# Two layer-norm and routing stages: half the normalization on ScalarE, a reordered addition, weight halves kept in DRAM, fewer filler products

## The reference, cut to what matters

```python
x = x + 0.5 * ffn(layernorm(x))          # "f1"
x = x + attention(layernorm(x))          # 16 heads of 8, relative positions
x = x + 0.5 * ffn(layernorm(x))          # "f2"

def ffn(x):
    normed = layernorm(x) * gamma + beta
    probs = softmax(normed @ router_w.T)             # 8 experts
    top_v, top_i = top_k(probs, 2); gates = softmax(top_v)
    out = sum over the 2 chosen experts of gate * (silu(g) * u) @ down_w[e].T   # 384 wide
    return out + shared_expert(normed)               # the same with 128, for every row
```

## Time and profile before

| | |
|---|---|
| median of 3 runs | 2171.59 us (2169.85 to 2174.17) |
| the profiled execution | 2175.47 us, of which the span 2173.70 us |
| TensorE busy | 2020.4 us (93%) |
| VectorE busy | 1906.4 us (88%) |
| ScalarE busy | 1292.8 us (59%) |
| GpSimd busy | 1257.7 us (58%) |
| mean granted clock of TensorE | 0.97 |

### The profile page before, as it was taken

How to read it: one execution, slowest core, us unless ns; L and a number is a source line. 1 busy time by engine, 2 the same in 40 slices (tenths; PEclk the granted TensorE clock), 3 DMA queues, 4 the chain that set the end, 5 groups by cost and what they waited for, 6 DMA issues and landing times. The chain is left out here.

```text
span 2173.7 us, 64335 instructions
## 1 busy us (share of the span) xinstructions
PE 2020.4 (93%) x22950; PEld 1228.5 (57%) x22951; DVE 1906.4 (88%) x4137; ACT 1292.8 (59%) x3126; POOL 1257.7 (58%) x1841
## 2 busy tenths in 40 slices
PE   7899999778999999999999999999999887999990
PEld 4589999533444444444444444444444465999990
DVE  7987666586999999999999999999999789877666
ACT  4455555376666666666666666666666354555550
POOL 3777775334555555556555555555565367777550
PEclk8999999899999999999999999999999899999995
DMA  5353222385021011202211210121000134322218
GB/s 165 91 134 88 86 83 64 105 258 143 2 41 41 7 36 41 39 4 41 41 29 14 41 41 7 36 60 41 2 7 7 56 106 130 105 88 85 72 50 234
DMA packets 163708, 147.86 MB, mean 68 GB/s; under 512 B 51858, under 2 KB 138002, under 8 KB 162898
## 3 DMA queue, kind: packets, MB, share of 16 engines
q1 hardware_dynamic: 144288, 108.31, 20.2%
q0 software_dynamic: 17280, 35.56, 4.8%
q10 hardware_dynamic: 1874, 0.51, 0.1%
HBM read 87.81 MB, written 60.45 MB: 68 GB/s over the span
## 5 line engine op out<-in xcount | busy, mean ns | idle before, releaser
L1330 PE MATMUL ps_scores<-c_relw,stat_rel 64*64 64x512 f32 x4096 | 937.4, 596 | 0.0
L1397 ACT ACTIVATE probs<-ps_scores,neg_max 128x512 f32<-128x512 f32 x1024 | 695.7, 684 | 396.1 <-DVE neg_max L1372 394.9
L1372 DVE TENSOR_REDUCE neg_max<-ps_scores 128x1 f32<-128x512 f32 x1024 | 645.4, 664 | 8.9 <-PE ps_scores L1330 7.9
L1365 DVE STREAM_TRANSPOSE probs_T<-probs 128x1024 f32<-128x1024 f32 x512 | 627.1, 1225 | 0.1
L1318 PE MATMUL ps_scores<-keys,stat_keys 64*64 64x512 f32 x2560 | 588.2, 595 | 0.5 <-ACT probs L1397 0.5
L1330 PEld LDWEIGHTS ps_scores<-c_relw,stat_rel 64*64 64x64 f32 x4096 | 278.5, 132 | 277.9 <-issue 209.3
L1318 PE MATMUL ps_scores<-c_batch,stat_keys 64*64 64x512 f32 x1536 | 352.6, 595 | 5.0 <-POOL stat_rel L1265 3.0
L1263 POOL TENSOR_TENSOR stat_keys<-queries_by_head,c_mask 128x128 f32<-128x128 f32 x320 | 152.5, 477 | 312.1 <-PE ps_scores L1330 312.1
L1290 PEld LDWEIGHTS ps_values<-probs_T,values_diag 128*32 128x32 f32 x8192 | 208.2, 109 | 205.3 <-issue 204.0
L1290 PE MATMUL ps_values<-probs_T,values_diag 128*32 128x128 f32 x8192 | 276.1, 276 | 1.1 <-DVE probs_T L1365 1.1
L1318 PEld LDWEIGHTS ps_scores<-keys,stat_keys 64*64 64x64 f32 x2560 | 171.5, 132 | 122.7 <-issue 112.6
(11 more groups left out here) (299 smaller groups left out, 3726.3 us busy)
## 6 DMA issues: line engine op xcount, KB each, us to landing
c_batch<-dispatched SPq DMA_DIRECT2D x142, 129.0 KB, 2.2
qkv_record<-f1c_rec SPq DMA_DIRECT2D x16, 768.0 KB, 3.9
f1c_Y<-expert_out SPq DMA_DIRECT2D x32, 256.0 KB, 4.4
f2c_Y<-expert_out SPq DMA_DIRECT2D x32, 256.0 KB, 3.9
c_batch<-qkv_record SPq DMA_DIRECT2D x24, 256.0 KB
keys<-qkv_record SPq DMA_DIRECT2D x20, 256.0 KB
attn_out_T<-attn_out SPq DMA_DIRECT2D x16, 256.0 KB, 2.0
c_Os<-attn_out_T SPq DMA_DIRECT2D x16, 256.0 KB, 3.4
```

The lines of the kernel that those rows point to most:

```text
L1330: m = nc.tensor.matmul(out, SR[n // 2 % NS][p, h, :, :].rearrange("p h a -> p (h a)"), R[p, w0:w0 + L], start=False, stop=True)
L1365: nc.vector.transpose(PT[G % 2][:, :, 2 * pair:2 * pair + 2, :, :].rearrange("p r i h a -> p r (i h a)"), Pr[U % NPAIR][:].rearrange("p i ...
L1372: nc.vector.reduce_max(nmx[U % NPAIR][:, n % 2:n % 2 + 1], psS[U % NPAIR][:, n % 2, :], AX, negate=True).then_inc(s_mx, 1)
L1397: nc.scalar.activation(Pr[s][:, n % 2, :], psS[s][:, n % 2, :], ACT.Exp, bias=nmx[s][:, n % 2:n % 2 + 1], accum_out=rs[:, G % 2, tt:tt + 1 ...
```

## The change

- `normalize` of odd steps goes to ScalarE. VectorE writes a `shift` of minus mean times reciprocal root for the step (`shifts`, one instruction of 128x4), ScalarE does four activations of 128x128 with it. In pairs 1 to 6 they stand between `high(a + 2)` and `gate(b)` of its program, in pair 0 behind `gate(b)`, and step 1 comes before everything.
- In f1 `shared(a - 1)` moves behind `next_stats(b + 2, b)`; in f2 it stays.
- f1 writes the finished halves of the weights to DRAM, 16 DMAs of 384 KB, one behind each row load of tiles 24 to 39. f2 loads them from there, 32 DMAs of 192 KB, without a wait among them for VectorE, and does neither `high` nor `low`.
- The `keep_busy` calls within the pairs go (10 and 6 products a pair in f1, 4 and 2 in f2). Those ahead of the first pair stay.
- SP's row loads from tile 24 on are written out, not looped.

```diff
             def load_weights(k):
+                if add_attention:
+                    for W, wd in zip((Wh, Wl), K["split"]):
+                        sp.dma_start(W[:, WCH * k:WCH * k + WCH], wd[:, WCH * k:WCH * k + WCH]).then_inc(s_kw, 16)
+                    return
...
+            def keep_weights(k):
+                W, wd = (Wh, Wl)[k % 2], K["split"][k % 2]
+                at = slice(2 * WCH * (k // 2), 2 * WCH * (k // 2 + 1))
+                sp.dma_start(wd[:, at], W[:, at].bitcast(F32)).then_inc(s_kw, 16)
...
-            run_steps(sp, NA, ET, NA, ET // XR8 * XR8, load_rows, XR8)
+            for n in range(NA, ET):
+                load_rows(Step(n // XR8, n % XR8, XR8))
+                if first and n - NA < NB:
+                    keep_weights(n - NA)
...
+            def shifts(s):
+                t = tokens(s)
+                wait(dve, (s_rs, KR * (s // 2) + KN))
+                stt(out=shift[:, t], in0=mv[:, t, 0], scalar=-1.0, in1=rs[:, t], op0=ALU.mult, op1=ALU.mult).then_inc(s_rs, 1)
...
             def low(s):
+                if add_attention:
+                    return
...
                 best(p, ch)
-                shared(a - 1)
+                if add_attention:
+                    shared(a - 1)
                 if more:
                     next_stats(b + 2, b)
                 else:
                     low(b)
+                if first:
+                    shared(a - 1)
                 choose(p, ch)
                 if more:
+                    shifts(b + 2)
                     normalize(a + 2)
-                    normalize(b + 2)
                     hidden(b)
...
             def high(s):
+                if add_attention:
+                    return
...
+            def normalize(s):
+                wait(act, (s_rs, KR * (s // 2 + 1)), (s_sc[s % 4], SC * ((s - NR) // 4 + 1)))
+                for j in range(JT):
+                    t = JT * s + j
+                    nc.scalar.activation(n0[0][s % NR][:, j, 0:D], XR[:, t, :], ACT.Identity, bias=shift[:, t:t + 1],
+                                         scale=rs[:, t:t + 1]).then_inc(s_Ca, 1)
...
                     if more:
                         high(a + 2)
+                        normalize(b + 2)
                     gate(b)
...
                     wait(pe, (s_D, KD * p + 2))
-                    keep_busy(10 if first else 4)
                     gate_up(b)
                     ranks(p)
...
-                keep_busy(6 if first else 2)
             down(NB - 1)
```

More of the change, by code:

```diff
@@ L216, in route @@
     with ExitStack() as c:
-        Wf = [sb(c, f"{tag}_Wgu{q}", [P, WCH]) for q in range(2)]
+        Wf = [sb(c, f"{tag}_Wgu{q}", [P, WCH]) for q in range(2)] if first else None
         if first:
@@ L223, in route @@
         rs = sb(c, tag + "_rs", [P, NT])
+        shift = sb(c, tag + "_shift", [P, NT])
         vf = sb(c, tag + "_vf", [P, JP])
@@ L268, in route @@
                            "rows", "gateup", "silu", "hidden", "down", "added", "whi", "wlo"))
-        s_nb, s_wd = S("copied"), S("wd")
+        s_nb, s_wd, s_Ca = S("copied"), S("wd"), S("normed_act")
+        s_kw = S("split")
         s_v, s_row, s_x, s_tab, s_G = (S(x) for x in ("map", "padrow", "padded", "tiletab", "gates"))
-        s_wf = [S(f"wf{q}") for q in range(2)]
+        s_wf = [S(f"wf{q}") for q in range(2)] if first else None
         s_sc = [S(f"scattered{q}") for q in range(4)]
@@ L362, in _ @@
                 sp.wait_ge(s_sc[q], SC * (NB // 4))
-            run_steps(sp, NA, ET, NA, ET // XR8 * XR8, load_rows, XR8)
+            if first:
+                sp.wait_ge(s_hi, NB)
+                sp.wait_ge(s_lo, NB)
+            for n in range(NA, ET):
+                load_rows(Step(n // XR8, n % XR8, XR8))
+                if first and n - NA < NB:
+                    keep_weights(n - NA)
+            if first:
+                sp.wait_ge(s_kw, 16 * NB)
         @block.gpsimd
@@ L479, in between @@
                 def between():
-                    if 0 < p and p + 1 < PAIRS and at[0] < KR:
+                    if 0 < p and p + 1 < PAIRS and at[0] < KN:
                         refine(p + 1, at[0])
@@ L502, in choose @@
                 ch(tt(DD[:, JP * p:JP * p + JP], v[:, 4, :], v[:, 3, :], ALU.subtract))
-                assert ch.k == KD and (p in (0, PAIRS - 1) or at[0] == KR)
+                assert ch.k == KD and (p in (0, PAIRS - 1) or at[0] == KN)
             def rows(p):
@@ L654, in _ @@
                     aggr(s, j)
-            for i in range(KR):
+            for i in range(KN):
                 refine(0, i)
+            shifts(1)
             normalize(0)
-            normalize(1)
             if first:
@@ L686, in _ @@
             next_stats(3, 1)
-            for i in range(KR):
+            for i in range(KN):
                 refine(1, i)
+            shifts(3)
             normalize(2)
-            normalize(3)
             hidden(1)
@@ L769, in gate @@
                 nc.scalar.activation(sg[s % 2][:], psG[:], ACT.Silu).then_inc(s_sg, 1)
+            normalize(1)
             for p in range(PAIRS):
@@ L809, in _ @@
             act.wait_ge(s_tab, 2)
-            act.wait_ge(s_lo, NB)
+            wait(act, (s_lo, NB) if first else (s_kw, 16 * 2 * NB))
             for k in range(2):
@@ L844, in transposes @@
             def transposes(s):
-                wait(pe, (s_C, KC * (s + 1)), (s_nT, s - 1))
+                wait(pe, ((s_C, s_Ca)[s % 2], KC * (s // 2 + 1)), (s_nT, s - 1))
                 for j in range(JT):
@@ L931, in _ @@
                     oproj(a + 4)
[L932 removed]
             down(NB - 1)
             pe.wait_ge(s_tab, 2)
[L936 removed]
+            wait(pe, (s_wd, 16), (s_wl, 1))
             wait(pe, (s_nT, NB), (s_D, KD * PAIRS), (s_E, KE * PAIRS))
```

18 lines of the change are left out of this document (11 added, 7 removed).

## The result

The changed kernel takes 2168.45 us (median of 20 runs), the kernel before 2172.65 us in the same session (20 runs). The ratio is 0.9979, with a 95% interval of 0.9972 to 0.9986, so 4.6 us less (3.0 to 6.1); the two medians differ by 4.2. The profiled execution took 2166.22 us with a span of 2164.4.

What follows compares the result with a forecast made beforehand. VectorE's list was taken as the dispatches' path, with extra cost when TensorE's clock falls. Terms 2.2 - 6.5 - 3.9 + 5.6 = -2.6 us on the 2171.6 us median gave 2169 us; own range 2165.5 to 2173, overall 2161 to 2181.

Steps and rivals of the forecast that it cites:

- Half the normalization to ScalarE: Both dispatches: gate(b) waits behind ScalarE's normalization, +0.32 us in pairs 1 to 6, less gains at the starts; +2.2 us.
- Halves from DRAM: Second dispatch: sixteen low subtractions of 0.45 us leave VectorE, 1.5 of them lost in front of waits; -6.5 us.
- The prediction's bound, -7.2: Second dispatch: all sixteen low subtractions, 0.45 us each, saved on VectorE; the other bound was -3.6 us.
- Shared addition behind statistics: First dispatch: the 6.3 us wait before shared(a-1) goes, some 2.4 come back before hidden(a); -3.9 us, bounds -6.3 and -2.5.
- Products of zeros: Both dispatches: without them 7 more falls of TensorE's clock at 0.8 us each; +5.6 us, bounds 0 and +19.7.
- the 48 us at which the count began: First dispatch: clock falls were counted from 48 us on, six pairs, two with a clock below 1.00, 0.33 per pair.
- The second dispatch's price of a fall: Second dispatch: pairs of 15.24 and 15.87 us against the undisturbed 14.67, so a fall costs 0.57 and 1.20 us.
- Writes, reads, written-out loads, 0: First tile stage and second dispatch: half writes, read-backs and unrolled loads don't reach TensorE or delay the first tile; 0 us.
- The clock holds: Rival, dispatches: clock falls stay at today's number, sum -8.2 us, 2163.4 us; chance 0.30.
- falls twice a pair: Rival, dispatches: clock falls behind the router's products and behind the wait for hidden(a), +11.5 us, 2183 us; chance 0.20.

Runs made afterwards that it cites:

- The two runs meant to show it: Kernel before with ScalarE half and written-out row loads, with products of zeros, then without: ratios 1.0017 and 0.9993 to the kernel before at 2451.74 us.
- The two edits tried together: Changed kernel with products of zeros back and gate(b) ahead of normalize(b + 2): ratio 0.9951 to the kernel before, 2162.61 against 2174.20 us.
- swapping two instructions: Changed kernel with gate(b) ahead of normalize(b + 2) in ScalarE's program: ratio 0.9968 to the kernel before.
- f2 makes halves: Changed kernel, but f2 makes the weight halves itself again and f1 writes none to DRAM: ratio 1.0021 to the kernel before.

## Why the prediction was right, by its steps

The forecast was 2169 us, 2.6 us less; 2168.45 and 4.6 less were measured. The total is right within its range, and in part by luck: the four terms as measured by undoing one part at a time would sum to -13.7 us, so the close total is not shown to come of four right terms. With the ratio 0.9979 as it stands, one of the four lies outside the error of its measurement (the shared addition) and one at its edge (the halves).

- **Half the normalization to ScalarE, +2.2.** The mechanism is shown: shift to `hidden(b)` was forecast at 2.38 with a wait of 1.1 to 1.2, and is 2.35 with 1.16 in the pair shown; four activations take 1.65. Over twelve pairs the wait is 1.28 on average and 1.71 at most, as the gate waits for TensorE in some. The experiment gives -0.9 with an error of 3.0, which holds +2.2 and zero alike.
- **Halves from DRAM, -6.5.** Measured -9.1, error 2.7. VectorE's list lost 6.9 us, as counted. The prediction's bound, -7.2, lies within the error; in the one profile idle time went along with the list, but whether a shorter list can give back more than its own length isn't shown.
- **Shared addition behind statistics, -3.9.** Mis-sized: -7.4, error 2.5. It isn't the assumption that 2.4 of the 6.3 us come back in front of `hidden(a)`: 1.95 do, in pair 1 and in the pair with the table. What the term left out is the rest of the pair: with the old order the waits before `best` and `hidden(b)` were longer, too. Taking the whole wait would have come nearer, for a wrong reason.
- **Products of zeros, +5.6.** +3.7, error 3.2, so the size is hardly tested. The reason was right in kind: the clock did fall more (0.90 to 0.84 in the first dispatch), and a fall in a middle pair does cost 0.8 to 0.9 us, against the 0.8 of the sum. What the profiles don't bear out is that the products keep these falls out: in the six pairs behind pair 1 the clock rose from 0.84 to 0.88 and the time stayed. The 3.7 us that the two profiles show lie in pair 1, ahead of the 48 us at which the count began, and a late weight block has about half of them. The second dispatch's price of a fall was also taken against its pair of 14.67 us alone. One of the pairs that the prediction leaves out took 16.28 at full clock, longer than the two at 0.89 from which the price comes:

```profile
1759.40:1775.68 16.28, 13.06 (x93) 9.83 (x92) 14.23 (x71) 8.07 (x16) 12.27 (x13) 1.00 0.36 106
```

- **Writes, reads, written-out loads, 0.** Shown by the tile stage, 276.3 us with and 276.2 without the writes.
- **Rivals.** "The clock holds" is excluded by 0.84, and "falls twice a pair" by the total and by pairs such as the one of 13.99 at 1.00. The Trainium skill, page "TensorE: Matmul & The Clock Gate", section "Why this matters for your kernels", warns of idle gaps between bursts of products, which cost the clock. The first dispatch's lower clock agrees; the pair of 13.99 us without products of zeros and still at 1.00 shows that not every pair of these lists has a gap that does.

Undone one at a time from the changed kernel, the parts come to 3.7 - 0.9 - 7.4 - 9.1 = -13.7 us, where -4.6 was measured. The gap of 9.1 us has an error of 6.6, since the ratio 0.9979 and its error are in all four prices. Two explanations are open.

- The parts are not additive. A guess that fits is that a part undone costs more when the products are gone, since each longer wait of TensorE then lets its clock fall (0.82 in the longer dispatch, in both kernels of the last two parts). The two runs meant to show it could not.
- The reference is off. The changed kernel was not run on the two chips of the single edits. If its ratio there were 0.9993 and not 0.9979, the parts would add up, at +6.7, +2.2, -4.3 and -6.1, close to the prediction's terms. That lies outside the interval measured in its own session (up to 0.9986), but no run on those chips tests it. The two edits tried together add up with 0.9979, with an error of some 5 us, which decides nothing.

What doesn't depend on it: with the shared addition or the halves alone undone, the kernel is slower than the kernel before in the same session. Each of the two is needed for the gain.

## What to carry over

When half of an operation moves to another engine, look at what stands behind it in that engine's queue: here 0.85 us of VectorE's work became 1.16 us of waiting for a gate that was held up by 1.55, and swapping two instructions only moved most of the wait to the next consumer. A wait in front of an instruction that can be moved behind 1.5 us of other work was worth its length or most of it. Before a stretch of one execution is taken as the price of an edit, look for something else that came late in it: here a weight block in pair 1, which accounts for about half of what the products of zeros seemed to win. And measure the kernel that all prices refer to in every session with the edits.

## What was not expected

- Two chips on which the first dispatch takes 1.6 times as long (212 for 130 us), with gaps of 0.5 to 1.9 us between VectorE's small instructions put down to issue or to no engine of the core, and the first tile stage 324 us for 276, while the attention stage is unchanged. The whole kernel took 2452 instead of 2174 us. What sets the stages apart isn't shown.
- The same dispatch in two executions differed by 2 to 3 us, with the granted clock (0.84 and 0.79 in the first dispatch of the changed kernel and of "f2 makes halves"). The changed kernel's 20 runs go from 2165.98 us at a mean clock of 0.967 to 2175.15 at 0.962. At this scale one profile cannot price an edit; the ratios of many runs can, with the reference among them.
